# Flamingo stack of four layers on one core: router with raw rows beside the projections, late attention steps of layer 0 with extra work behind their own, and outputs sorted by expert number

## The reference, cut to what is computed

```python
x = x + tanh(g_xattn[l]) * xattn_l(layernorm(x), ctx)
x = x + tanh(g_ffn[l]) * ffn_l(layernorm(x))
# ffn_1 (ffn_2: RMS norm times norm_weight in front, hidden 512, and x added to what comes out)
logits = x_flat @ Wr                      # 2048 x 8
w, ind = top_k(logits, 2)
w = softmax(w)
combine = one_hot(ind) weighted by w      # 2048 x 8
for each expert: out += combine[:, e] * (gelu(x_flat @ W1e + b1e) @ W2e + b2e)
```

## Time and profile before

| | before |
|---|---|
| median of 3 runs | 1629.38 us (1626.49 to 1644.27) |
| the profiled execution | 1641.02 us |
| its span in the trace | 1639.2 us |
| granted TensorE clock, mean | 0.919 |
| busy share: PE, DVE, ACT, POOL | 81%, 59%, 53%, 40% |

### The profile page before, as it was taken

How to read it: one execution, slowest core, us unless ns; L and a number is a source line. 1 busy time by engine, 2 the same in 40 slices (tenths; PEclk the granted TensorE clock), 3 DMA queues, 4 the chain that set the end, 5 groups by cost and what they waited for, 6 DMA issues and landing times.

```text
span 1639.2 us, 29178 instructions
## 1 busy us (share of the span) xinstructions
PE 1331.4 (81%) x9489; PEld 956.7 (58%) x9516; DVE 970.1 (59%) x2674; ACT 866.6 (53%) x1720; POOL 656.5 (40%) x719
## 2 busy tenths in 40 slices
PE   1798799988996679999986699846799867995986
PEld 1454489745553568999964355525678534554433
DVE  6798653438868423333345588662455447876797
ACT  2366654336883335555533388543455334885564
POOL 4566330116510575565035473027743435623000
PEclk9999899997998789999998699968899987998998
DMA  9997030289812323533145995113553569940001
GB/s 290 285 146 116 2 113 1 93 212 171 128 22 84 121 77 123 200 133 107 40 120 160 231 133 74 52 47 121 155 190 104 158 192 186 128 60 1 0 14 39
DMA packets 144175, 189.63 MB, mean 116 GB/s; under 512 B 21937, under 2 KB 110385, under 8 KB 143985
## 3 DMA queue, kind: packets, MB, share of 16 engines
q0 software_dynamic: 79264, 103.35, 32.5%
q1 hardware_dynamic: 64768, 84.41, 15.9%
HBM read 128.96 MB, written 50.99 MB: 110 GB/s over the span
## 4 chain that ended last, share of the span: by engine, by line
PE 52%; DVE 15%; DMA 8%; issue 7%; ACT 6%; POOL 6%; another core or an unknown queue 4%; SPq 0%; DVEq 0%; ACTq 0%; POOLq 0%
PE PS L1129 10%; PE PS L1109 8%; PE PS L960 6%; PE PS L903 5%; PE PS L930 3%; PE PS L1121 3%; DMA stack<-mt 2%; DVE nm L2026 2%; DMA qk_parts<-q_parts 2%; POOL x_res L610 1%; PE PS L940 1%; PE PS L997 1%; DVE st L1744 1%; POOL wslot L770 1%
## 5 line engine op out<-in xcount | busy, mean ns | idle before, releaser
L2026 DVE TENSOR_REDUCE nm<-PS 128x2 f32<-128x512 f32 x384 | 251.4, 679 | 48.1 <-PE PS L903 48.0
L1129 PE MATMUL PS<-weights,hh 128*128 x936 | 192.0, 295 | 31.2 <-DVE hl L2324 29.3
L1109 PE MATMUL PS<-weights,xh 128*128 x468 | 172.1, 422 | 13.9 <-issue 5.8
L903 PE MATMUL PS<-stack 48*128 48x256 f32 x1024 | 142.0, 359 | 42.7 <-DVE nm L2026 12.8
L1129 PEld LDWEIGHTS PS<-weights,hh 128*128 128x128 f32 x936 | 154.4, 195 | 35.3 <-issue 34.7
L633 POOL DMA_DIRECT2D stack<-mt x128 | 71.7, 560 | 225.2 <-ACT mt L1443 222.6
L1434 ACT ACTIVATE probs<-PS 128x512 f32<-128x512 f32 x256 | 138.9, 594 | 42.8 <-PE PS L930 21.3
L903 PEld LDWEIGHTS PS<-stack 48*128 48x128 f32 x1024 | 85.5, 206 | 127.8 <-issue 65.2
L1434 ACT ACTIVATE xng<-PS 128x512 f32<-128x512 f32 x256 | 139.0, 595 | 38.4 <-PE PS L940 14.4
L1601 ACT ACTIVATE hh<-PS 128x512 fp32r<-128x512 f32 x117 | 65.8, 596 | 176.3 <-PE PS L1121 134.4
L1129 PE MATMUL PS<-weights,hl 128*128 x468 | 134.2, 287 | 0.0
(11 more groups left out here) (315 smaller groups left out, 3110.4 us busy)
## 6 DMA issues: line engine op xcount, KB each, us to landing
stack<-qk_parts POOLq DMA_DIRECT2D x128, 256.0 KB, 4.2
qk_parts<-stack SPq DMA_DIRECT2D x32, 512.0 KB
qk_parts<-q_parts SPq DMA_DIRECT2D x32, 512.0 KB, 8.8
stack<-qk_parts POOLq DMA_DIRECT2D x128, 128.0 KB, 3.7
weights<-W_dram POOLq DMA_DIRECT2D x12, 1024.0 KB, 7.7
ys_sorted<-yo SPq DMA_DIRECT2D x78, 128.0 KB
wide<-ctxT_dram SPq DMA_DIRECT2D x16, 512.0 KB, 6.5
weights<-W_dram POOLq DMA_DIRECT2D x12, 512.0 KB, 5.6
```

Source lines behind the costliest of these rows:

```text
L903: mm = pe.matmul(PS[:, (2 * t + h) % 3, qt * S:(qt + 1) * S], q[rows, qt * P:(qt + 1) * P], kk[rows], start=True, stop=True)
L1109: add = lambda x, w: pe.matmul(PS[:, hid_bank(p) + h, :], x[:, p, c, :], w, start=False, stop=True, skip_group_check=True)
L1129: add = lambda x, w: pe.matmul(o, x, w, start=False, stop=True, skip_group_check=True)
L2026: nc.vector.tensor_reduce(nm[:, j % 2, at:at + 2], PS[:, (2 * t + h) % 3, :].rearrange("p (q n) -> p q n", q=2), AX.X, ALU.max, negate=Tru ...
```

## The change

It has three parts.

*Router.* PE transposes raw rows of `x_res` in place of normalised ones, for three of the four groups between the projections, and multiplies them with centred gate weights: PE sums each column of the weights (`router_means`), DVE takes the mean off (`centre`), and for layer 2 multiplies by `norm_w` ahead of it. The two largest logits keep their order under a positive scale per token, so DVE multiplies just their difference by the token's scale. For layer 2 the two roots of a half are taken in one instruction. Pool, no longer DVE, makes the normalised rows that go to memory (`normalise`), groups 0 and 1 after the first half's scales, groups 2 and 3 after the second half's.

*Late steps of layer 0.* ACT's extra work stands behind the step's own and, for `highs`, a little later; Pool's first two `lows` come one step later and DVE's `light_scales` one step earlier.

*Outputs by expert number.* A token's two outputs are now ordered by expert number: `plan` works with the minimum and the maximum of the two (`gt` 8 and 9), and Pool's `by_expert` swaps the weights where needed and works out which stores to wait for. All 16 outputs of the lower expert are gathered once the tiles up to expert 6 are stored, and Pool scales them itself (`scale_lower`, four gathers behind); the 16 of the higher expert follow once the tiles up to expert 7 are stored. DVE adds the lower ones without a weight (`add_lower`) and the higher ones with it (`add_higher`).

```diff
@@ ACT, attend
-                    if l == 0 and ffn(0):
-                        if n in (25, 26):
-                            highs(0, n - 25)
-                        if n == 27:
-                            light_root(0)
-                        if n in (28, 29):
-                            highs(1, n - 28)
-                        if 30 <= n < 34:
-                            light_normed(2 * n - 60)
-                            light_normed(2 * n - 59)
                     if 0 <= k < QUADS:
                         exps(l, 2 * k)
...
                     if n >= TIMES_V:
                         take_pv(l, n - TIMES_V)
+                    if l == 0 and ffn(0):
+                        if n == 26:
+                            light_root(0)
+                        if n in (27, 28):
+                            highs(0, n - 27)
+                        if n in (29, 30):
+                            highs(1, n - 29)
+                        if 31 <= n < 35:
+                            light_normed(2 * n - 62)
+                            light_normed(2 * n - 61)
@@ POOL, attention steps
-                    if l == 0 and ffn(0) and n in (28, 29):
-                        lows(0, n - 28)
+                    if l == 0 and ffn(0) and n in (29, 30):
+                        lows(0, n - 29)
@@ PE, behind out_project(l, b)
+                        if l in (1, 2) and ffn(l):
+                            if b == 1:
+                                router_means(l)
+                            if b in (2, 4, 6):
+                                transposes(u + 1, b // 2 - 1)
+                            if b in (4, 6, 7):
+                                router(l, (b - 3) // 2)
@@ DVE, add_out
+                    if halved and b == 2:
+                        centre(l)
+                    if halved and b == CUTS + 2:
+                        half_scales(2 * l + 1, 0)
@@ DVE, route
+                then(nc.vector.tensor_tensor(gt[:, 2, :], gt[:, 2, :], sml[:, 8 if l == 1 else 11, :], ALU.mult))
@@ POOL, ahead of the gathers of tokens
+                    def normalise(g):
+
+                        u, xn = 2 * l + 1, xn_slot(2 * l + 1, g)
+                        for t in range(4):
+                            at = 4 * g + t
+                            ins = nc.gpsimd.tensor_scalar(xn[:, t, :], x_res[:, at, :], mv[:, at, 0:1],
+                                                          sml[:, 8 if l == 1 else 11, at:at + 1], ALU.subtract, ALU.mult)
+                        ins.then_inc(xn_ready, 1)
+                    pool.wait_ge(o_done, QUADS * (l + 1))
+                    for h in range(2):
+                        pool.wait_ge(ln_v[2 * l + 1], HALF[2 * l + 1] * (h + 1))
+                        if h == 1:
+                            pool.wait_ge(xo_done[l], B)
+                            for e in range(2):
+                                load_biases(e)
+                        normalise(2 * h)
+                        normalise(2 * h + 1)
@@ POOL, gathers of outputs
-                    for p in range(2):
-                        pool.wait_ge(ys_out[p], 16 * ((NT + 1 - p) // 2) * l)
-                    for k in range(FED[l]):
-                        if k >= 8:
-                            pool.wait_ge(y_done[l], added(k - 8))
-                        nc.gpsimd.indirect_dma_start(yg[:, k, :], None, ys,
-                                                     bass.IndirectOffsetOnAxis(pos[:, k % 2, k // 2:k // 2 + 1], 0)
-                                                     ).then_inc(yg_in[k % 8], 16)
+                    by_expert(l)
+                    for m in range(2):
+                        for p in range(2):
+                            at = 8 + 2 * p + m
+                            pool.wait_ge(ys_out[p], pool.value_load(upto_e[0:1, at:at + 1], min_val=16, max_val=16 * (NT + 1)))
+                            nc.gpsimd.tensor_tensor(gone[:, 1 + 2 * m + p:2 + 2 * m + p], zero[:], zero[:], ALU.add)
+                        for t in range(TILES):
+                            nc.gpsimd.indirect_dma_start(yg[:, 2 * t + m, :], None, ys,
+                                                         bass.IndirectOffsetOnAxis(pos[:, m, t:t + 1], 0)
+                                                         ).then_inc(yg_in[t // 2], 16)
+                            if m == 0 and t >= LAG:
+                                scale_lower(l, t - LAG)
+                            if m == 1 and t < LAG:
+                                scale_lower(l, TILES - LAG + t)
@@ SP, load_ternary
-                sp.wait_ge(y_done[2], 24)
+                sp.wait_ge(y_done[2], TILES + 12)
```

More of the change, by code:

```diff
@@ L370, in stored, with count_before @@
             return out[n % 2], 32 * (n // 2 + 1)
+        def count_before(u, g, what):
+            if u == 0:
+                return 8 * g + (0 if what == "variances" else 2)
+            if what == "variances":
+                return (0, 2, 10, 18)[g]
+            return (4, 12, 20, 26)[g]
         def rows_of(n, r, g):
@@ L382, in fed @@
             return (yo_done, NT * l) if l in (1, 2) else (y_done[l], FED[l])
-        def added(k):
-            return k // 4 * 4 + (1, 3, 2, 4)[k % 4]
         def xn_slot(u, g):
@@ L779, in transposes @@
             def transposes(u, g):
-                pe.wait_ge(xn_ready, GROUPS * u + g + 1)
+                if u in HALVES:
+                    pe.wait_ge(xo_done[u // 2], 2 * g + 2)
+                else:
+                    pe.wait_ge(xn_ready, GROUPS * u + g + 1)
                 at = xT_bank(u, g)
@@ L999, in out_project, with router_means @@
                 mm.then_inc(wo_mm, 1)
+            def router_means(l):
+                pe.wait_ge(wg_in, 16 * l)
+                pe.wait_ge(o_done, QUADS * (l + 1))
+                if l == 2:
+                    pe.wait_ge(route_v[l], 1)
+                for kc in range(KC):
+                    mm = pe.matmul(PS[:, 7, 0:EXPERTS], ones[:], wg[:, kc, :], start=(kc == 0), stop=(kc == KC - 1))
+                mm.then_inc(lg_mm, 1)
             def router(l, g):
                 if g == 0:
-                    pe.wait_ge(wg_in, 16 * l)
+                    pe.wait_ge(route_v[l], 2)
                 else:
@@ L1526, in norm @@
                 for c in range(KC):
-                    ins = nc.scalar.activation((x0h if l == 0 else nT if l == 3 else xnT)[:, c, at],
-                                               PS[:, xT_bank(u, g) + c, :], ACT.Identity,
-                                               scale=col("norm_w", c) if l == 2 else 1.0)
+                    ins = nc.scalar.activation(xrT[:, g, c, :] if l in (1, 2) else (nT if l else x0h)[:, c, at],
+                                               PS[:, xT_bank(u, g) + c, :], ACT.Identity)
                 ins.then_inc(xT_done, 1)
@@ L1685, in _ @@
                             split_high(l, b // CUTS, b % CUTS)
+                            if b in (3, 5, 7):
+                                norm(l, (b - 3) // 2)
+                            if b in (5, 7):
+                                logits(l, (b - 5) // 2)
                 if not ffn(l):
@@ L2069, in attend, with centre @@
                             light_variances(0)
-                        if ffn(0) and n == 28:
+                        if ffn(0) and n == 27:
                             light_scales(0)
-            def add_out(l, more):
+            def centre(l):
+                dve.wait_ge(lg_mm, (GROUPS + 1) * (l - 1) + 1)
+                for kc in range(KC):
+                    ins = nc.vector.scalar_tensor_tensor(wg[:, kc, :], PS[:, 7, 0:EXPERTS], -1.0 / D, wg[:, kc, :], ALU.mult, ALU.add)
+                    if l == 1 or kc == KC - 1:
+                        ins.then_inc(route_v[l], 1)
+            def add_out(l, more):
+                if l == 2 and ffn(l):
+                    dve.wait_ge(wg_in, 32)
+                    for kc in range(KC):
+                        ins = nc.vector.tensor_scalar(wg[:, kc, :], wg[:, kc, :], col("norm_w", kc), None, ALU.mult)
+                    ins.then_inc(route_v[l], 1)
                 for b in range(B):
@@ new lines, in sparse @@
+                if l == 1:
+                    add_lower(*range(12))
+                    keys_low(l + 1, 0)
+                    add_lower(*range(12, TILES))
+                    add_higher(0)
+                    keys_low(l + 1, 1)
+                else:
+                    keys_low(l + 1, 0)
+                    add_lower(*range(12))
+                    keys_low(l + 1, 1)
+                    add_lower(*range(12, TILES))
+                    add_higher(0)
+                add_higher(1)
+                group_scales(2 * l + 2, 0)
@@ L2376, in sparse @@
+                keys_low(l + 1, 2)
+                add_higher(2)
+                group_scales(2 * l + 2, 1)
+                keys_low(l + 1, 3)
+                add_higher(3)
+                group_scales(2 * l + 2, 2)
+                queries(l + 1, 0)
```

(1 more changed line is left out.)

224 lines of the change are left out of this document (107 added, 117 removed).

## The result

The changed kernel ran in 1625.62 us (median of 12, 1619.09 to 1633.39), the kernel before beside it in 1631.22 (median of 12). The ratio is put at 0.9944, 95% interval 0.9921 to 0.9967, so the change gains 9 us (5 to 13). That is not the quotient of the two medians, which is 0.9966 or 5.6 us, at the edge of the interval. The forecast was 1599 us, ratio 0.981, range 1582 to 1620: the sign was right, the size was not, and the time lies outside the range.

The account below looks back on a forecast made before the run. Bounds were waits in layer 0's attention, the router's serial tail and late gathers and K stores behind the experts. Terms -8.3 - 2.2 - 15 - 5 = -30.5 on 1641.02, ratio 0.981 of median 1629.38: 1599 us, range 1582 to 1620.

Parts of the forecast that it names:

- Late steps, -8.3 us: Layer 0's attention: moving ACT's weight copies and Pool's addition gains 8.3 us, bounds 0 and -11.
- Both terms: Layer 0: ACT's step shrinks from 10.58 to 3.82 (6.76 us); Pool's addition leaves DVE's 128x512 instruction (1.51 us).
- The case of 3.398 us: Layer 0: the worst DVE 128x512 time; 2.65 us more gained if Pool's addition meets no DVE instruction.
- Router, -2.2 us: Router of layers 1 and 2: -0.2 and -3.2 us, plus 1.2 for added DVE instructions; bounds -8 and 0.
- The 36.3 us to the last logits: Router, both layers: forecast stretch from first projection to last logits, with transposes and matmuls moved between projections.
- I cost them at nothing because the plan hides them: Pool's 16 layernorm instructions per layer beside router and plan: cost 0, or 7.5 us per layer without that cover.
- The row for a Pool TENSOR_SCALAR: Profile row: a 1.22 us two-input DVE instruction ran inside Pool's 3.69 us one; so new Pool work costs DVE nothing.
- Rival C: Router plan, layers 1 and 2: Pool's normalisations block DVE's two-input instructions, 15 us, giving 1614; chance 0.13.
- Outputs by expert number, -15 and -5 us: Early gathers between layers 1 and 2 gain 15 us (bounds 0, -24), between 2 and 3 gain 5 (0, -16).
- D: Behind the experts: gathers were not the limit, only the first two parts count, -10.5, giving 1619; chance 0.16.
- E: Last six expert tiles: early gathers slow their output stores; at 24.5 us per store, 1683; chance 0.06.
- B: Behind the experts: first K store no longer slowed, -24 and -13 instead of -15 and -5, 1582 us; chance 0.15.

Follow-up runs that it names:

- e1: Only the late steps of layer 0 put on the kernel before; ratio 0.9941, -9.7 us.
- e2: Only the router part put on the kernel before; ratio 1.0025, +4.1 us.
- e14: Only the outputs by expert number put on the kernel before, later tensors padded to multiples of 64 bytes; ratio 0.9935.
- e13: The kernel before with one small tensor padded so that later tensors lie 64 bytes further; ratio 1.0054.
- e7: The whole change, but DVE instead of Pool weights the lower experts' rows and gathers of four tiles share a semaphore; ratio to the kernel before 0.9948.
- e9: The kernel before with one small tensor enlarged so that later tensors lie 32 bytes further; ratio 1.0071.
- e17: The kernel before with later tensors 32 bytes further, measured once more beside an unchanged copy; ratio 1.0088.
- e4: The whole change once more, beside its three parts on the same chip; ratio to the kernel before 0.9919.
- e11: The whole change again, beside a version with later tensors at multiples of 64 bytes; ratio to the kernel before 0.9989, 1576.0 us.
- e16: The kernel before itself, unchanged, measured as if it were another; ratio 1.0019.

## Why the prediction was wrong, point by point

- **What bounds the kernel.** Most waits were read rightly: the stages of layer 0 and behind the experts got shorter by their removal. The router's stretch hardly did, from 36.5 to 36.4 us in layer 1.
- **Late steps, -8.3 us.** Right: -9.7 (e1). Both terms are there. The two steps at the earlier trace rows take 8.7 us in place of 14.8, 6.1 of the 6.76. The step beside the DVE instruction of the earlier trace rows took 5.5 to 6.9 us in the nine traces without this part and takes 4.2 in the eleven with it, 1.3 to 2.7 us where 1.51 was forecast. The case of 3.398 us from the earlier trace rows is another instruction, at 195.69, beside which ACT's step is 4.1 us in both kernels.
- **Router, -2.2 us.** Wrong in two terms: +4.1 (e2). The 36.3 us to the last logits came out at 36.4 in layer 1 and 38.3 in layer 2 (37.1 to 38.3 over all traces), so layer 2 gained 1.3 us in the two traces and not 3.2. The step that failed is "I cost them at nothing because the plan hides them". The plan does hide their duration, but it grows by 2.9 us per layer. The row for a Pool TENSOR_SCALAR that leaves DVE alone was of the wrong sort: one DVE instruction of 128x1024, where the plan is some forty small ones, of which about a dozen are stretched. Rival C had put 15 us on it; it was 5.8 for both layers, the added instructions among it. The lock of which the Trainium skill tells ("SBUF — State Buffer", section "SBUF: two separate sides") is held for a whole instruction, against DVE instructions in a 2-port mode or with two SBUF inputs. The trace shows two-input instructions stretched, up to 0.48 us, and a TENSOR_SCALAR of 8 elements with one input at 0.40 instead of 0.17 us, whose mode it does not show; none was blocked for the 1.2 us of a Pool instruction.
- **Outputs by expert number, -15 and -5 us.** In the stages it was about right: -14.4 and -10.2 us at the level of the profiled runs, less 2.3 and 4.1 for tiles 33 to 35, together -18.2. At equal addresses it measured -19.5 (e14 against e13). The split was off, and so was the reason given for layers 2 to 3: K of group 2 was thought held "until about 1321.43 as before". It is copied at 1300.80, and Pool's chain of scalings and gathers is what comes before it (e7). At the quicker level this stretch gains just 1.8 us.
- **What the sum left out.** The two enlarged tensors were read in the change and costed at nothing, not even named. The shift cost 9 to 14 us in the kernel before by the ratios and 7 to 10 by the medians (e9, e13, e17), as much as the whole gain measured. This is the step that made the prediction wrong, with 6 us from the router.
- **The parts together.** With -9.7, +4.1, -19.5 and some +9 to +11 for the shift the sum is -14 to -16. Measured were -9 (the result), -13 (e4) and at the other level -2 (e11, or -6 by the medians; there the two stretches gain 12 us in place of 25). A few us of this stay open.
- **Rivals.** D's number, 1619, is nearest to the result, by coincidence: the gathers' gain, which D denied, was there and was lost elsewhere. C's mechanism was there at two fifths of its price. E's 1683 was excluded by its own condition, stores of 24.5 us, and what was seen of it is 6.4 us. B's -13 for layers 2 to 3 is nearer to the -10.2 than the forecast's -5; its -24 for layers 1 to 2 is not.
- **The range** ended at 1620 because each bound was taken from a mechanism of the three parts. None of them covered a cost outside the moved instructions, and the profiled execution, 10 us above the later median of its own kernel, had no part in the range.

## What to carry to other kernels

Before costing a change, look at whether it moves the addresses of the large SBUF tensors, and measure the padding alone; putting new small tensors behind the large ones should avoid the shift, which was not tried here. An engine that takes work off another is not free beside a chain of many small instructions: count them, and not just the durations. Gathers may start on partial results when tokens can be ordered by when their rows are complete, but here that order without the early start was 2% slower than the kernel before.

## What the runs showed of the hardware

- The same 79264 packets of the software queue took 32.5 to 33.8% of the DMA engines' time at one layout of SBUF and 35.7 to 38.7% when the tensors declared behind two small ones lay 32 to 128 bytes further. In the kernel before, the time rose by 0.5 to 0.9% with 32 and 64 bytes (e9, e13, e17).
- Eight Pool TENSOR_SCALARs of 128x256, which take 0.94 us each in the earlier trace rows, took 9.79 us beside DVE's plan, 1.22 each, and DVE's small instructions beside them up to 0.48 instead of 0.17.
- One program ran at two levels, 1580 and 1636 us, on the same chip on different occasions. Between the traces of the kernel before and of its copy e16, 64.5 us apart, the first 12 tiles account for 17 us in layer 1 (97.4 and 80.8 us) and 23 in layer 2 (67.7 and 44.6), and the two stretches behind the experts for 16.
